# Score products of a four-layer cross-attention kernel cut into 32x32 tiles of TensorE, with mask tables in both forms

## The reference

```python
# layer 0 (attention 0: self, causal; attention 1: context)
energy = jnp.einsum('bhsk,bhtk->bhst', Q, K)
lengths = jnp.sum(energy[:, :, 0, :] != 0, axis=-1)
energy = jnp.where(cols[None, None, None, :] >= lengths[:, :, None, None], -jnp.inf, energy)
if causal:
    energy = jnp.where(cols[None, :] > cols[:, None], -jnp.inf, energy)
score = jax.nn.softmax(energy / jnp.sqrt(jnp.asarray(dk, energy.dtype)), axis=-1)
out = jnp.einsum('bhst,bhtk->bhsk', score, V) * m
...
# layer 1 (attention 2: self, with a 128x128 mask; attention 3: context, with a mask per batch)
scores = jnp.einsum('bhqd,bhkd->bhqk', Q, K) / math.sqrt(DK)
scores = jnp.where(mask == 0, jnp.float32(-1000000000.0), scores)
attn = jax.nn.softmax(scores, axis=-1)
out = jnp.einsum('bhqk,bhkd->bhqd', attn, V)
...
# layer 2 (attention 4: context, 16 heads of 64), layer 3 (attention 5: context, 16 heads of 16)
```

## Time and profile before

| what | value |
|---|---|
| median of 3 runs | 2317.47 us |
| profiled execution, its own time | 2318.61 us |
| its span, first to last instruction | 2316.8 us |
| mean granted TensorE clock | 0.999 of 2.4 GHz |
| TensorE matmul busy | 2298.6 us, 99% |
| TensorE weight loads busy | 1980.0 us, 85% |
| VectorE, ScalarE, GpSimd busy | 65%, 60%, 41% |
| instructions in the span | 74,091, of them 30,353 matmul and 30,353 weight-load records |

### The profile page before, as it was taken

The page is one execution under the profiler, slowest core; times in us unless marked ns, Lnnn a source line. Parts: engine busy times, 40 slices in busy tenths (PEclk is TensorE's granted clock), DMA queues, the critical chain, the costliest instruction groups (busy, mean ns, idle before and its releaser), DMA issues.

```text
span 2316.8 us, 74091 instructions
## 1 busy us (share of the span) xinstructions
PE 2298.6 (99%) x30353; PEld 1980.0 (85%) x30353; DVE 1513.0 (65%) x3091; ACT 1386.6 (60%) x3238; POOL 956.7 (41%) x1764
## 2 busy tenths in 40 slices
PE   8999999999999999999999999999999999999998
PEld 7888898888888888888888888888888888888887
DVE  7977654456897665445789776445478977544456
ACT  5566665455567666555656766555465666655555
POOL 3574322233457432223345743223334674322233
PEclk9999999999999999999999999999999999999999
DMA  4400000000100000000010000000001000000000
GB/s 159 143 3 3 2 2 1 1 1 18 37 7 3 3 2 2 1 1 1 25 32 5 3 3 2 2 1 1 1 28 31 4 3 3 2 2 1 1 1 20
DMA packets 23793, 32.51 MB, mean 14 GB/s; under 512 B 2304, under 2 KB 22176, under 8 KB 23328
## 3 DMA queue, kind: packets, MB, share of 16 engines
q1 hardware_dynamic: 23456, 27.78, 3.7%
HBM read 23.57 MB, written 4.19 MB: 12 GB/s over the span
## 4 chain that ended last, share of the span: by engine, by line
PE 98%; issue 0%; DVE 0%; ACT 0%; DMA 0%; POOL 0%; SPq 0%; POOLq 0%; ACTq 0%; DVEq 0%
PE M L583 55%; PE SC L779 16%; PE M L589 12%; PE M L813 7%; PE SC L795 3%; PE M L830 3%; PE SC L627 2%; ACT Pr L985 0%; DMA W<-w_k 0%; DVE nmax L1219 0%; DMA X<-x 0%; PE M L721 0%; POOL Kx L1340 0%; ACT Qx L955 0%; POOL rstd L1388 0%
## 5 line engine op out<-in xcount | busy, mean ns | idle before, releaser
L583 PE MATMUL M<-XT,W 128*128 128x128 f32 x4096 | 511.8, 276 | 0.9 <-DMA W<-w_k 0.9
L583 PEld LDWEIGHTS M<-XT,W 128*128 128x128 f32 x4096 | 496.9, 193 | 17.3 <-issue 11.5
L1219 DVE TENSOR_REDUCE nmax<-SC 128x8 f32<-128x1024 f32 x320 | 390.8, 1221 | 157.1 <-PE SC L779 154.5
L1388 POOL TENSOR_SCALAR rstd<-mv 128x1 f32<-128x1 f32 x256 | 111.8, 437 | 665.5 <-DVE mv L1291 665.5
L985 ACT ACTIVATE Pr<-SC 128x1024 f32<-128x1024 f32 x256 | 262.1, 1024 | 190.6 <-PE SC L779 189.3
L779 PE MATMUL SC<-Qx,Kx 32*128 32x128 f32 x5120 | 372.0, 283 | 0.3 <-issue 0.3
L779 PE MATMUL SC<-Kx,Qx 32*128 32x128 f32 x5120 | 364.5, 280 | 2.1 <-issue 0.4
L779 PEld LDWEIGHTS SC<-Kx,Qx 32*128 32x128 f32 x5120 | 315.9, 186 | 58.8 <-issue 56.3
L779 PEld LDWEIGHTS SC<-Qx,Kx 32*128 32x128 f32 x5120 | 310.7, 186 | 2.5 <-issue 0.9
L1340 POOL TENSOR_SCALAR Kx<-K,own,k_ones 128x128 f32<-128x128 f32 x640 | 286.5, 460 | 23.6 <-PE SC L779 19.8
L955 ACT ACTIVATE Qx<-M,q_bias,q_scale 128x128 f32<-128x128 f32 x640 | 240.9, 457 | 69.7 <-PE M L583 68.1
(11 more groups left out here) (145 smaller groups left out, 4089.7 us busy)
## 6 DMA issues: line engine op xcount, KB each, us to landing
X<-x SPq DMA_DIRECT2D x32, 128.0 KB, 2.3
c_in<-ctx_in SPq DMA_DIRECT2D x32, 128.0 KB, 2.1
out<-X SPq DMA_DIRECT2D x32, 128.0 KB, 1.8
RV<-row_vec SPq DMA_DIRECT2D x1, 2304.0 KB, 8.9
W<-w_k SPq DMA_DIRECT2D x5, 256.0 KB, 3.8
W<-w_q SPq DMA_DIRECT2D x5, 256.0 KB, 4.3
W<-w_v SPq DMA_DIRECT2D x5, 256.0 KB, 4.2
W<-w_f SPq DMA_DIRECT2D x1, 1024.0 KB, 7.1
```

The lines of the kernel that those rows point to most:

```text
L583: last = pe.matmul(dst, a, b, start=(k == 0), stop=(k == len(lhsTs) - 1))
L1219: dve.tensor_reduce(nm, SC[h][:, :].rearrange("p (g c t) -> p g c t", c=KC, t=P), AX_X, ALU.max, negate=True).then_inc(maxima, 1)
```

## The change

Three edits. The score products of all narrow steps are issued in four pieces of 32 output rows each (`cols = 32`), so that masks and products have the same 32x32 tile shape. For that the mask tables are kept in both forms in every group of 32 partitions (128 x 2 x 4 x 128 each), and a unit's masks use the row groups that its products use. And to keep within SBUF, `c_in` and `q0` have one buffer instead of two, with the waits and the place of the context load in SP's list to match.

```diff
-        put("SP", slot(b, 0) - 2.0, "context", b)
+        put("SP", slot(b, 0) - 0.75, "context", b)
...
-        causal_t, mask_ss_t = sb("causal_t", [P, 4, P], BF16), sb("mask_ss_t", [P, 4, P], BF16)
+        causal_t, mask_ss_t = sb("causal_t", [P, 2, 4, P], BF16), sb("mask_ss_t", [P, 2, 4, P], BF16)
...
-        c_in, CmT = ring(2, "c_in", [P, D]), ring(2, "CmT", [P, D])
+        c_in, CmT = ring(1, "c_in", [P, D]), ring(2, "CmT", [P, D])
...
-        q0 = ring(2, "q0_", [P, 2, P])
+        q0 = ring(1, "q0_", [P, 2, P])
...
-                    if b >= 2:
-                        sp.wait_ge(tile_full, done("tile", ("CT", b - 2)))
+                    if b >= 1:
+                        sp.wait_ge(tile_full, done("tile", ("CT", b - 1)))
...
-                for u, first in ((s_u, 0), (t_u, 2)):
+                for form, u in enumerate((s_u, t_u)):
                     if mask_table(u) is not None:
-                        parts += [(mask_table(u), SC[u % 2], e, first + e) for e in range(2)]
+                        parts += [(mask_table(u)[:, form], SC[u % 2], e, 2 * (u % 2) + e) for e in range(2)]
...
-                for which in range(2):
-                    mask, bank = whole(which), SC[0][:, which * 512:(which + 1) * 512]
-                    for j in range(4):
-                        for i in range(4):
-                            rows = [ident_b[:, 32 * j:32 * j + 32], mask] if i < 2 else [mask[:, 32 * j:32 * j + 32], ident_b[:, :]]
-                            last = pe.matmul(bank[32 * i:32 * i + 32, j * P:(j + 1) * P], rows[0], rows[1], start=True,
-                                             stop=True, skip_group_check=True)
-                last.then_inc(causal_turned, 1)
+                for which in (1, 0):
+                    mask = whole(which)
+                    for form in range(2):
+                        bank = SC[1 - which][:, form * 512:(form + 1) * 512]
+                        for j in range(4):
+                            rows = [mask[:, 32 * j:32 * j + 32], ident_b[:, :]] if form else [ident_b[:, 32 * j:32 * j + 32], mask]
+                            for i in range(4):
+                                last = pe.matmul(bank[32 * i:32 * i + 32, j * P:(j + 1) * P], rows[0], rows[1],
+                                                 start=True, stop=True, skip_group_check=True)
+                    last.then_inc(causal_turned, 1)
...
-                    once(tables_done, 1)
+                    once(tables_done, 1 if s_u == 0 else 2)
...
+                    cols = 32
                     for i in range(max(len(line) for line in lines)):
                         for at, (line, starting) in enumerate(zip(lines, starts)):
                             if i < len(line):
                                 dst, lhsT, rhs = line[i]
-                                filled[at] = pe.matmul(dst, lhsT, rhs, start=(starting and i == 0),
-                                                       stop=(i == len(line) - 1), skip_group_check=True)
+                                for c in range(0, P, cols):
+                                    filled[at] = pe.matmul(dst[c:c + cols], lhsT[:, c:c + cols], rhs,
+                                                           start=(starting and i == 0), stop=(i == len(line) - 1),
+                                                           skip_group_check=True)
...
-                for i, table in enumerate((mask_ss_t, causal_t)):
-                    last = act.activation(chunks(table[:, :, :].rearrange("p j n -> p (j n)")),
-                                          chunks(SC[0][:, i * 512:(i + 1) * 512]), ACT.Copy)
-                last.then_inc(tables_done, 1)
+                for i, table in enumerate((causal_t, mask_ss_t)):
+                    act.wait_ge(causal_turned, i + 1)
+                    act.activation(table[:, :, :, :].rearrange("p f j n -> p (f j n)"), SC[i][:, :],
+                                   ACT.Copy).then_inc(tables_done, 1)
...
-                    if i >= 2:
-                        pool.wait_ge(tile_full, done("tile", ("L", INDEX["q0"][i - 2])))
+                    if i >= 1:
+                        pool.wait_ge(tile_full, done("tile", ("L", INDEX["q0"][i - 1])))
```

More of the change, by code:

```diff
@@ L424, in build @@
         x_loaded, stored = [sem(f"x_loaded{i}") for i in range(LANES)], [sem(f"stored{i}") for i in range(LANES)]
-        c_loaded, m_loaded = [sem(f"c_loaded{i}") for i in range(2)], sem("m_loaded")
+        c_loaded, m_loaded = sem("c_loaded"), sem("m_loaded")
         ready_act, ready_dve, scales_done = sem("ready_act"), sem("ready_dve"), sem("scales_done")
@@ L510, in load_context @@
             def load_context(b):
-                sp.dma_start(c_in[b % 2][:, :], ctx_in[b, :, :]).then_inc(c_loaded[b % 2], 16)
+                sp.dma_start(c_in[0][:, :], ctx_in[b, :, :]).then_inc(c_loaded, 16)
             sp.dma_start(Pr[0][:, 0:C_COLS], consts[:, :]).then_inc(consts_in, 16)
@@ L693, in _ @@
                     b = it[1]
-                    pe.wait_ge(c_loaded[b % 2], 16 * (b // 2 + 1))
-                    turn(tile_of(it), c_in[b % 2], KC).then_inc(tile_full, 1)
+                    pe.wait_ge(c_loaded, 16 * (b + 1))
+                    turn(tile_of(it), c_in[0], KC).then_inc(tile_full, 1)
                 elif kind == "BT":
@@ L881, in keep_tables @@
             def keep_tables():
-                act.wait_ge(causal_turned, 1)
-                for i, table in enumerate((mask_ss_t, causal_t)):
-                    last = act.activation(chunks(table[:, :, :].rearrange("p j n -> p (j n)")),
-                                          chunks(SC[0][:, i * 512:(i + 1) * 512]), ACT.Copy)
-                last.then_inc(tables_done, 1)
+                for i, table in enumerate((causal_t, mask_ss_t)):
+                    act.wait_ge(causal_turned, i + 1)
+                    act.activation(table[:, :, :, :].rearrange("p f j n -> p (f j n)"), SC[i][:, :],
+                                   ACT.Copy).then_inc(tables_done, 1)
                 act.wait_ge(cols_in, 16)
@@ L1040, in _ @@
                 dve.memset(nmax[i][:, :], 0.0)
-                dve.memset(q0[i][:, :, :], 0.0)
+            dve.memset(q0[0][:, :, :], 0.0)
             dve.wait_ge(consts_in, 16)
```

## The result

The changed kernel takes 2746.81 us (median of 4 runs, 2738.68 to 2753.58) against 2318.0 us of the kernel before on the same chip: ratio 1.185, interval 1.181 to 1.188. That is 429 us slower, where the prediction had 207. The profiled execution took 2753.58 us with a span of 2751.7.

The account below looks back on a forecast made before the run. TensorE, 99% busy, bounds the kernel; after the change its instruction pages bind. Profiled 2318.6 + 168 (array's gain included) + 40 under the loads = 2526.6, less 1.1 to the median: 2525 us, range 2288 to 2750.

Parts of the forecast that it names:

- The change in the array: a gain of 21 us: Score steps on TensorE: one shape for masks and scores saves 16.7 us, closer passes 4.7 us; bounds 0 to 40 us.
- Streaming itself doesn't shrink: Score products: four 32x32 tiles stream in the same 0.11 us as one 32x128 tile, so no change there.
- 7 ns: Score steps: spacing assumed between starts of neighbouring 32-column score records.
- The 0.11 us behind masks: Masked steps: delay from masks to scores that one tile shape removes, 152 x 0.11 = 16.7 us gained.
- Rival 3: Score steps: sequencer hands out records no faster than 15 ns each, 4.4 us a masked step, about 2700 us; chance 0.05.
- Pages: TensorE's instruction packets, about 252 records each, arrive late once records double: 168 us in four rounds plus 40 under loads.
- F: Floor on time per instruction page: packet start delay plus 2.35 us; estimated 3.55 us, 6.4 under the loads.
- Rival 1: Instruction pages never bind, eight held ahead or start delay vanishing; array's gain stands alone, 2296 us; chance 0.17.
- the same laying: New record list laid over old start times, no page sooner than F after the last: 42 us a round.
- 288 records of a masked step: Masked steps: 32 + 256 records in 1.1 us exceed a page, so the page there takes F.
- The small edits: Single context and q0 buffers, mask tables in both forms: 0, within 2 us; under 10 us if cover failed.
- Rivals 2 and 4: Small page floor, 2310 to 2322 us, chance 0.04; only four f32 tiles overlap in score steps, 3190 us, chance 0.03.

Follow-up runs that it names:

- experiments 5 and 6: Four f32 products of 512 columns put ahead of each score step, in the kernel before and in the changed kernel: 3496.42 and 3713.93 us.
- experiment 11: Kernel before with ten blocks of products at its end, 8 to 16 tiles a round: 2392.62 us in one run, only the trace counts.
- experiment 9: Changed kernel, but score steps of the first eight narrow slots keep tiles of 128 columns: 2688.5 us, ratio 1.1609 to the kernel before.
- experiment 8: Changed kernel with 32-column tiles only in steps that have mask tables, 128 columns elsewhere: 2532.08 us, ratio 1.0930 to the kernel before.
- experiment 10: Kernel before with 96 small bf16 products ahead of each of the 335 score steps, score products untouched: 2824.25 us, ratio 1.2175.
- experiment 1: Changed kernel with score products as one 128-column tile again, the other edits kept: 2317.26 us, ratio 0.9995 to the kernel before.
- experiments 4 and 5: Kernel before with nine blocks of unread matmuls at its end, 2421.43 us; kernel before with four 512-column f32 products ahead of each score step, 3496.42 us.
- experiment 2: Changed kernel with score pieces of 64 columns instead of 32: 2332.61 us, ratio 1.0064 to the kernel before.

## Why the prediction was wrong

**What failed: "The change in the array: a gain of 21 us".** It measured a loss of 210 to 217 us (the table of steps, experiments 5 and 6), outside the bounds of 0 to 40 us gain. Two sentences of that step fail. "Streaming itself doesn't shrink: four 32x32 tiles of a row group do the work of one 32x128 tile in the same 0.11 us" is true of one round, not of the next: a round of 16 tiles takes 0.43 us, not 0.22. And only the first products start "7 ns" apart; the others follow at 16.7 ns and, as a round of 16 takes 0.43 and not 0.27 us, with pauses between. The 0.11 us behind masks was right (the transition fell from 0.31 to 0.18 us) and drowned in four rounds of 0.2 us.

**The rival that was closest was rejected on too short evidence.** Rival 3 (a rate of records in the steps) got 0.05 because "seven or more records started within 0.02 us" and 32 mask records within 0.05. Both are bursts out of the stock of 64 instructions; neither tells what happens behind it. Its size was wrong too (4.4 us a step, measured 2.1), for a step that had taken 1.47 us in the old form said nothing of the limit. 16.7 ns for an f32 product is 8.3 ns a matmul record. Nor is a rate alone the answer (experiment 11).

**Pages: right in kind; near in size, but partly by luck: 229 us forecast (168 net of the 21 us gain, and 40), 212 measured** (429 - 217.5). F where DMA is quiet is 3.47 us (3.55 estimated); a late page's first record runs 2.2 to 2.9 us behind its packet; the wide attention stays at 165 us; 485 packets. Rival 1 (eight pages of room) is refuted in this case: TensorE waits at page heads, 118 us in 125 times at the score line alone. The first 100 us of the old kernel: some 45 us in and outside the steps, of which 33 go with experiment 9; 40 were forecast, for pages alone. The steps hold about 10 of the 45, the waits 22 and the clock of 0.92 about 12.

**The luck: the same laying, with steps of their true length, would have given less.** Longer steps give pages more time. Laid again over the records with these lengths (an estimate), F = 3.55 us leaves 45 to 80 us for pages and 3.8 us 90 to 120, by how the first 100 us are priced. There were 212. Of them 144 are visible waits for issue and about 47 the half clock behind them, which the prediction did not have; some 21 are left, which may lie in waits that the modelled ends of products cover. Why the waits are 144 us and not 45 to 120 stays open: experiment 8 missed its range by the same kind of gap. The half clock was read from the profile and not tested by itself; with filling between the steps it was not there (0.999), and the four runs of experiment 10 bear out its price.

**A reading that was loose.** The prediction has the 288 records of a masked step "in 1.1 us". That is the score products alone; with the masks the step had taken 1.47 us, and it now takes 2.11.

**The small edits** were right: 0 (experiment 1). Rivals 2 and 4 are out (experiments 4 and 5).

The sum as measured: 217 in the steps + 144 waiting at page heads + about 47 at half clock + about 21 not placed = 429.

No version beats both kernels: the only gain seen, 58 ns in each of 27 one-sided steps with 64 columns (experiment 2), would be 1.6 us, less than can be measured.

## What to carry to other kernels

Before packing f32 products more finely, count tiles in use times instructions: up to 8 f32 tiles a round nothing was lost here; with 16 tiles of 128 columns the second eight brought next to nothing. Count the records per us as well: where more than some 250 fell into 3.5 us here, TensorE waited for its own instructions, and behind some of these pauses its clock was at the lower level. A burst at the start of a group is no proof of a rate; look for a stretch of over 64 instructions, or make one.

## What was not expected of the hardware

- A round of 16 f32 tiles takes its two passes and some 0.2 us, whatever the pass (0.43, 0.647, 1.073 us at 128, 256, 512 columns); bf16 on 16 tiles loses nothing at 512 columns (0.216 us) and takes 0.133 us a round at 128.
- After a first burst (6.7 ns a product in f32), f32 products start 16.7 ns apart in long stretches, bf16 products 8.33 ns.
- A full 128x128 array with 32 columns a product went at 25 ns each, and with that a page's floor shows as a gap of 0.28 us in every 128 matmuls.
- A wait of 1.9 us from record to record (1.60 idle) was followed by some 3 us in which records of 256 columns started 427 ns apart, the rate of the lower clock level.
